# A graph network's closing layer: batch statistics taken about the first group's mean while the tiles are made, and the last norm's square and product on ScalarE with a bias and scale of each partition

## The reference, cut to what matters

```
h = (1.0 + eps[0]) * x + aggr                       # aggr: mean over incoming edges
out = jax.nn.relu(h @ w1 + b1) @ w2 + b2
out = out + (x @ res_w + res_b)
mean = jnp.mean(out, axis=0)                        # over the 6250 nodes, one for each feature
var = jnp.var(out, axis=0)
out = (out - mean) * jax.lax.rsqrt(var + BN_EPS) * gamma + beta
x = _layernorm(x + jax.nn.relu(out), axis=-1)       # _layernorm: (x - m) / sqrt(v + 1e-5) over the 128 features
```

## Time and profile before

| | us |
|---|---|
| median of 3 runs | 8809.26 |
| lowest, highest | 8806.7, 8819.43 |
| the profiled execution, own time | 8815.13 |
| its span, first to last instruction | 8813.4 |

### The profile page before, as it was taken

How to read it: one execution, slowest core, us unless ns; L and a number is a source line. 1 busy time by engine, 2 the same in 40 slices (tenths; PEclk the granted TensorE clock), 3 DMA queues, 4 the chain that set the end, 5 groups by cost and what they waited for, 6 DMA issues and landing times. The chain is left out here.

```text
span 8813.4 us, 60467 instructions
## 1 busy us (share of the span) xinstructions
PE 2052.3 (23%) x16367; PEld 1898.9 (22%) x16367; DVE 5593.5 (63%) x10159; ACT 3091.3 (35%) x3341; POOL 6086.1 (69%) x6351
## 2 busy tenths in 40 slices
PE   5776634555400000810000720000500000300002
PEld 5666634555300000710000610000400000200002
DVE  7665546766599998868888468888632222432225
ACT  6333312333266665345555345555200000100002
POOL 2777777777777775667776367777267776577773
PEclk5555555555555555955555865555555555555556
DMA  4621114444366665656665556666333332233331
GB/s 131 216 60 42 37 51 134 130 133 135 115 204 219 218 216 180 206 195 216 216 216 201 170 192 216 216 216 211 93 95 105 105 105 95 78 106 105 105 105 56
DMA packets 496250, 1288.01 MB, mean 146 GB/s; under 512 B 153909, under 2 KB 262024, under 8 KB 428968
## 3 DMA queue, kind: packets, MB, share of 16 engines
q1 hardware_dynamic: 236712, 755.83, 24.3%
q0 software_dynamic: 229248, 473.78, 18.5%
q10 hardware_dynamic: 29952, 54.54, 2.4%
HBM read 731.68 MB, written 551.98 MB: 146 GB/s over the span
## 5 line engine op out<-in xcount | busy, mean ns | idle before, releaser
L1405 POOL DMA_INDIRECT l_swp_G<-table,KVI x1664 | 1576.4, 947 | 512.3 <-issue 506.7
L1661 POOL DMA_INDIRECT l2s_G<-table,OTHI x832 | 786.7, 946 | 388.1 <-issue 253.3
L1661 POOL DMA_INDIRECT l3s_G<-table,OTHI x832 | 787.7, 947 | 301.5 <-issue 253.3
L1065 POOL DMA_INDIRECT arrived<-plc_QS,plc_idx x832 | 812.3, 976 | 253.5 <-issue 244.3
L1065 POOL DMA_INDIRECT slots<-REC,plc_idx x832 | 798.5, 960 | 273.1 <-issue 251.7
L1150 POOL DMA_INDIRECT l_G<-table,OTHI x832 | 790.1, 950 | 256.1 <-issue 253.0
L904 PE MATMUL plc_pr<-plc_seen,plc_otf 128*128 128x49 f32 x3328 | 861.5, 414 | 12.4 <-DVE plc_seen L674 12.4
L904 PEld LDWEIGHTS plc_pr<-plc_seen,plc_otf 128*128 128x128 f32 x3328 | 846.6, 326 | 32.1 <-issue 31.9
L1508 DVE SCALAR_TENSOR_TENSOR l_swp_QS<-l_swp_QS,KEEP,l_swp_QX 128x128 f32<-128x128 f32 x1664 | 588.3, 354 | 45.9 <-DMA l_swp_QX<-queries 8.6
L1617 PE MATMUL l_swp_AW<-l_swp_ET,ones 128*128 128x512 f32 x4 | 4.1, 1140 | 2155.2 <-DVE l_swp_ET L1597 2155.2
L1287 DVE TENSOR_TENSOR_SCAN l_X<-l_AW,l_X 128x2244 f32<-128x2244 f32 x104 | 502.5, 4831 | 3.6
(11 more groups left out here) (491 smaller groups left out, 9633.2 us busy)
## 6 DMA issues: line engine op xcount, KB each, us to landing
sums<-l_ROW SPq DMA_DIRECT2D x104, 1088.0 KB, 4.6
l_swp_QX<-queries SPq DMA_DIRECT2D x104, 1088.0 KB, 8.3
sums<-l_swp_ROW SPq DMA_DIRECT2D x104, 1088.0 KB, 5.2
queries<-plc_zrow SPq DMA_DIRECT2D x55, 1088.0 KB
plc_QX<-queries SPq DMA_DIRECT2D x104, 544.0 KB, 4.2
l_A<-arrived SPq DMA_DIRECT2D x52, 1056.0 KB, 7.7
sums<-l3s_ROW SPq DMA_DIRECT2D x52, 1032.0 KB
plc_low<-low_rows ACTq DMA_DIRECT2D x208, 256.0 KB, 3.6
```

The lines of the kernel that those rows point to most:

```text
L1065: pool.indirect_dma_start(out=slots, out_offset=bass.IndirectOffsetOnAxis(ap=idx[:, c % IB, j:j + 1], axis=0), in_=g.REC[:, c * CH + j, :] ...
L1405: pool.indirect_dma_start(out=G[:, c % GR, j, :], out_offset=None, in_=table, in_offset=bass.IndirectOffsetOnAxis(ap=index[:, c * CK + j:c ...
L1661: pool.indirect_dma_start(out=G[:, c % GR, j, :], out_offset=None, in_=table, in_offset=bass.IndirectOffsetOnAxis(ap=g.OTHI[:, c * CK + j: ...
```

## The change

Batch statistics. TensorE's sum of every tile in the loop (L2660) is kept for the first seven tiles only; their sum, divided by 7 x 128, is the mean of the first group (the same PSUM bank, now read as pp). From step 7 on, once in seven steps, VectorE adds its negative to one group of HH (part(G), between keep and mix; the first also reads pp), ScalarE squares that group at the head of its next step (square(G)), and TensorE, at the end of the step after, sums both the shifted group and its squares (total(G), 14 matmuls). The seventh group's part, square and total stand behind the loop. The variance is then the mean of the squares less the square of the mean, both about the shifted origin, and gamma, beta and the remaining mean are folded into one scale and one offset for each feature.

The last norm. VectorE's group-wide subtraction (L2581) and product (L2590) go. ScalarE squares tile by tile with the negative mean as a bias of each partition (seven instructions for a group), and multiplies tile by tile with Identity, scale and bias of each partition (seven more). VectorE gets one small operation more in second(G), and first(G) begins, from G = 2, with a wait for the norm of group G-2.

```
@@ names and buffers @@
...
-        stat = s.sb("stat", [P, 2, D])
-        st = s.sb("st", [P, 2, 3, GT])
+        stat = s.sb("stat", [P, 4, D])
+        st = s.sb("st", [P, 2, 4, GT])
+        pp = pm
@@ sync @@
-                sp.wait_ge(normed, G + 1)
+                sp.wait_ge(normed, (G + 1) * GT)
@@ -2551,43 +2553,54 @@
                 v.wait_ge(done, n + 1)
                 v.tensor_tensor(HH[:, n, :], po[:, n % 2, 0:D], g.RES[:, n, :], ALU.add).then_inc(kept, 1)
+            def part(G):
+                if G == 0:
+                    v.wait_ge(pivoted, 1)
+                    link(v.tensor_scalar(stat[:, 0, :], pp[:, 0:D], -1.0 / (GT * P), None, ALU.mult))
+                v.tensor_tensor(HH[:, group(G), :], HH[:, group(G), :], flat(stat[:, 0, :]), ALU.add).then_inc(parted, 1)
             for q in range(GT):
                 mix(q)
             for s_ in range(-3, NB):
                 if 0 <= s_ + 1 < NB:
                     keep(s_ + 1)
+                if s_ >= GT and (s_ + 1) % GT == 1 and s_ // GT - 1 < NG - 1:
+                    part(s_ // GT - 1)
                 mix(s_ + 3 + GT)
-            v.wait_ge(totalled, 1)
-            link(v.tensor_scalar(stat[:, 0, :], pm[:, 0:D], 1.0 / N, None, ALU.mult))
             v.wait_ge(kept, NB)
-            for G in range(NG):
-                v.tensor_tensor(HH[:, group(G), :], HH[:, group(G), :], flat(stat[:, 0, :]), ALU.subtract).then_inc(parted, 1)
+            part(NG - 1)
             v.wait_ge(varied, 1)
-            v.tensor_scalar(stat[:, 1, :], pv[:, 0:D], 1.0 / N, 1e-5, ALU.mult, ALU.add).then_inc(ready, 1)
+            link(v.tensor_scalar(stat[:, 2, :], pm[:, 0:D], 1.0 / N, None, ALU.mult))
+            link(v.tensor_tensor(stat[:, 3, :], stat[:, 2, :], stat[:, 2, :], ALU.mult))
+            link(v.tensor_scalar(stat[:, 1, :], pv[:, 0:D], 1.0 / N, 1e-5, ALU.mult, ALU.add))
+            v.tensor_tensor(stat[:, 1, :], stat[:, 1, :], stat[:, 3, :], ALU.subtract).then_inc(ready, 1)
             v.wait_ge(rooted, 1)
             link(v.reciprocal(stat[:, 1, :], stat[:, 1, :]))
             link(v.tensor_tensor(stat[:, 1, :], stat[:, 1, :], par[:, 0, :], ALU.mult))
+            link(v.tensor_tensor(stat[:, 2, :], stat[:, 2, :], stat[:, 1, :], ALU.mult))
+            link(v.tensor_tensor(stat[:, 2, :], par[:, 1, :], stat[:, 2, :], ALU.subtract))
             def first(G):
                 h, x, m = HH[:, group(G), :], g.X[:, group(G), :], st[:, G % 2, :, :]
-                if G == 0:
-                    v.wait_ge(squared, NG)
+                if G >= 2:
+                    v.wait_ge(normed, (G - 1) * GT)
                 link(v.tensor_tensor(h, h, flat(stat[:, 1, :]), ALU.mult))
-                link(v.tensor_tensor(h, h, flat(par[:, 1, :]), ALU.add))
+                link(v.tensor_tensor(h, h, flat(stat[:, 2, :]), ALU.add))
                 link(v.scalar_tensor_tensor(out=x, in0=h, scalar=0.0, in1=x, op0=ALU.max, op1=ALU.add))
                 link(v.tensor_reduce(m[:, 0, :], x, AX.X, ALU.add))
-                link(v.tensor_scalar(m[:, 0, :], m[:, 0, :], -1.0 / D, None, ALU.mult))
-                v.tensor_tensor(x, x, cols3(m[:, 0, :]).to_broadcast(wide), ALU.add).then_inc(centered, 1)
+                v.tensor_scalar(m[:, 0, :], m[:, 0, :], -1.0 / D, None, ALU.mult).then_inc(centered, 1)
             def second(G):
-                x, m = g.X[:, group(G), :], st[:, G % 2, :, :]
-                v.wait_ge(squared2, G + 1)
+                m = st[:, G % 2, :, :]
+                v.wait_ge(squared2, (G + 1) * GT)
                 link(v.tensor_reduce(m[:, 1, :], SQ[:, G % 2, :, :], AX.X, ALU.add))
                 v.tensor_scalar(m[:, 1, :], m[:, 1, :], 1.0 / D, 1e-5, ALU.mult, ALU.add).then_inc(spread, 1)
                 v.wait_ge(rooted2, G + 1)
                 link(v.reciprocal(m[:, 2, :], m[:, 2, :]))
-                v.tensor_tensor(x, x, cols3(m[:, 2, :]).to_broadcast(wide), ALU.mult).then_inc(normed, 1)
+                v.tensor_tensor(m[:, 3, :], m[:, 0, :], m[:, 2, :], ALU.mult).then_inc(scaled, 1)
             for G in range(NG + 1):
                 if G < NG:
@@ -2598,7 +2611,16 @@
         @block.scalar
         def _(act):
             act.wait_ge(loaded, 96)
+            def square(G):
+                act.wait_ge(parted, G + 1)
+                if G >= 2:
+                    act.wait_ge(totalled, G - 1)
+                act.activation(SQ[:, G % 2, :, :], HH[:, group(G), :], ACT.Square).then_inc(squared, 1)
             for s_ in range(-3, NB):
+                if s_ >= GT + 1 and s_ % GT == 1 and s_ // GT - 1 < NG - 1:
+                    square(s_ // GT - 1)
                 n = s_ + 3
                 if n < NB:
                     act.wait_ge(turned, n + 1)
@@ -2611,20 +2633,29 @@
                     if n >= 2:
                         act.wait_ge(done, n - 1)
                     act.activation(zt[:, n % 2, :], pz[:, n % 2, 0:P], ACT.Relu, bias=b1[:, 0:1]).then_inc(bent, 1)
-            for G in range(NG):
-                act.wait_ge(parted, G + 1)
-                if G >= 2:
-                    act.wait_ge(totalled, G)
-                act.activation(SQ[:, G % 2, :, :], HH[:, group(G), :], ACT.Square).then_inc(squared, 1)
+            square(NG - 1)
             act.wait_ge(ready, 1)
             act.activation(stat[:, 1, :], stat[:, 1, :], ACT.Sqrt).then_inc(rooted, 1)
+            def squares(G):
+                act.wait_ge(centered, G + 1)
+                for j in range(GT):
+                    act.activation(SQ[:, G % 2, j, :], g.X[:, G * GT + j, :], ACT.Square,
+                                   bias=st[:, G % 2, 0, j:j + 1]).then_inc(squared2, 1)
+            def norm(G):
+                act.wait_ge(scaled, G + 1)
+                for j in range(GT):
+                    act.activation(g.X[:, G * GT + j, :], g.X[:, G * GT + j, :], ACT.Identity,
+                                   bias=st[:, G % 2, 3, j:j + 1], scale=st[:, G % 2, 2, j:j + 1]).then_inc(normed, 1)
             for G in range(NG + 1):
                 if G < NG:
-                    act.wait_ge(centered, G + 1)
-                    act.activation(SQ[:, G % 2, :, :], g.X[:, group(G), :], ACT.Square).then_inc(squared2, 1)
+                    squares(G)
                 if G >= 1:
                     act.wait_ge(spread, G)
                     act.activation(st[:, (G - 1) % 2, 2, :], st[:, (G - 1) % 2, 1, :], ACT.Sqrt).then_inc(rooted2, 1)
+                    norm(G - 1)
         @block.tensor
         def _(pe):
@@ -2633,6 +2664,13 @@
             def ones_of(n):
                 return g.ones if n < NB - 1 else valid
+            def total(G):
+                pe.wait_ge(squared, G + 1)
+                for n in range(G * GT, (G + 1) * GT):
+                    pe.matmul(pm[:, 0:D], ones_of(n)[:, :], HH[:, n, :], start=(n == 0), stop=(n == NB - 1))
+                    o = pe.matmul(pv[:, 0:D], ones_of(n)[:, :], SQ[:, G % 2, n % GT, :], start=(n == 0), stop=(n == NB - 1))
+                o.then_inc(totalled if G < NG - 1 else varied, 1)
             for s_ in range(-3, NB):
                 n = s_ + 3
@@ -2655,17 +2693,14 @@
                         pe.wait_ge(kept, n - 1)
                     pe.matmul(po[:, n % 2, 0:D], zt[:, n % 2, :], w[:, 1, :], start=True, stop=True).then_inc(done, 1)
                 n = s_
-                if n >= 0:
+                if 0 <= n < GT:
                     pe.wait_ge(kept, n + 1)
-                    o = pe.matmul(pm[:, 0:D], ones_of(n)[:, :], HH[:, n, :], start=(n == 0), stop=(n == NB - 1))
-            o.then_inc(totalled, 1)
-            for n in range(NB):
-                G = n // GT
-                if n % GT == 0:
-                    pe.wait_ge(squared, G + 1)
-                o = pe.matmul(pv[:, 0:D], ones_of(n)[:, :], SQ[:, G % 2, n % GT, :], start=(n == 0), stop=(n == NB - 1))
-                if n % GT == GT - 1:
-                    o.then_inc(totalled if n < NB - 1 else varied, 1)
+                    o = pe.matmul(pp[:, 0:D], g.ones[:, :], HH[:, n, :], start=(n == 0), stop=(n == GT - 1))
+                    if n == GT - 1:
+                        o.then_inc(pivoted, 1)
+                if s_ >= GT + 2 and s_ % GT == 2 and s_ // GT - 1 < NG - 1:
+                    total(s_ // GT - 1)
+            total(NG - 1)
 class Args:
```

More of the change, by code:

```diff
@@ L2474, in close_all @@
             "chain", "loaded", "made_v", "mixed", "turned", "copied", "made", "bent", "done", "kept", "totalled"))
-        parted, squared, varied, ready, rooted, centered, squared2, spread, rooted2, normed, stored = (s.sem(x) for x in (
-            "parted", "squared", "varied", "ready", "rooted", "centered", "squared2", "spread", "rooted2", "normed", "stored"))
+        parted, squared, varied, ready, rooted, centered, squared2, spread, rooted2, normed, stored, pivoted, scaled = (
+            s.sem(x) for x in ("parted", "squared", "varied", "ready", "rooted", "centered", "squared2", "spread", "rooted2",
```

(1 more changed line is left out.)

## The result

The changed kernel takes 8840.1 us (median of 7 runs, 8838.19 to 8843.5) against 8807.19 us before (7 runs), a ratio of 1.0037, 95% interval 1.0028 to 1.0046: 33 us slower. The forecast was 8836, +26.6 us. The profiled execution took 8843.5 us with a span of 8841.8, against 8813.4.

A forecast was written before the change was run, and what follows sets the result against it. GpSimd's fetches were taken to bound the kernel up to 8716 us, then close_all's chain of waits. Terms 20.1 - 7.1 + 11.6 + 2 gave +26.6 us, the median going from 8809.3 to 8836, range 8814 to 8853.

The forecast's parts named there:

- rival 1: Making stage hides its additions, TensorE's total running under VectorE's mixes: 8814 us, no change that can be measured; chance 0.13.
- Rivals 2 and 4: 2: first(G)'s wait falls under other work, 8789 us, chance 0.03. 4: Identity forces function table loads, 8854 us, chance 0.04.
- Term 1: Making stage: in-order queues behind square and total stretch a cycle to 11.7 us, last keep at 8752.3; +20.1 us.
- term 4: TensorE's clock in the making stage: one total falling under the low clock costs 0 to 3.1 us; put at +2.
- Rival 3: Clock stays at 0.50 for most of the making stage, a cycle near 15 us: 8868, half of it 8852; chance 0.10.
- Term 2: Statistics, from the last keep to the last norm: 9.1 us where it was 16.2; -7.1 us.
- Term 3: Last norm: squares, Sqrt and norm form a chain with nothing beside it, 10.5 us a group against 8.5; +11.6 us.

The follow-up runs named there:

- the statistics alone: The change's batch statistics with the last norm of before, against the kernel before on the same chip: ratio 1.0035 (1.0006 to 1.0065), +26.8 us from the third group's first mix.

## Why the prediction was right

**In short.** The order of the queues was read rightly in both halves; one term, the clock, was sized wrong; and that the total came so near was part luck. The stage lost 36.4 us where the sum had 26.6, and the medians are only 33 apart; what makes up the 3.5 between isn't shown.

**What bounds, and the rivals.** The stage left the fetches' pace and was bound by its own order from the first part on, as said: mixes of the third group on came 14.8, 14.1, 13.3 and 14.0 us apart in the first result, and all of rival 1 is refuted by its own mark (the next group's first mix started 14.8 us behind its forerunner, not 8.7). Rivals 2 and 4 did not occur; the trace has no table load in close_all, and from the end of Sqrt to the first product are 0.47 us, which leave no room for one of 1.283.

**Term 1, the making stage.** Mechanism right, each hop of the cycle of rows above within 0.1 us but one: the total. The step that was off is term 4, the clock: one fall at +2 us, where every total in the loop met the low level, 29.7 us in place of 18.7. That is 11 us of the 11.9 by which the stretch passed 20.1. Its own signs say the same: VectorE's idle time was to be 2.5 to 3.5 us and was 4.8 to 5.7 behind every total; the last keep was to be near 8752, 87.6 us behind the first mix, and was 99.5 behind it. Rival 3 (the low clock for most of the stage) had the right cause and too high a price: from the first part to the last keep the clock was low for 31 of 77 us. The forecast had the warning in its hand, one block and longer gaps, and weighed it as a single accident.

**Term 2, the statistics.** -5.4 for -7.1: the last total took 5.0 us, at a granted clock of 0.66, where the first total of the statistics alone, at 1.00, took 3.3; the rest as counted. Without that the stretch is 9.2 us in four of the experiments, against 9.1 worked out.

**Term 3, the last norm.** +9.8 for +11.6. The prices were right (squares 2.15 for 7, one starting every 0.29; products 2.80 for 7, one every 0.39 with scale and bias), and so were both waits, 2.87 for norm and 1.12 for Sqrt. (The 0.09 for an operand came from two rows that differ also in the input's type, bf16 against f32; the 0.29 and 0.39 measured here bear it out.) The period was 10.26 for 10.5, some hops of 0.04 and a link counted too many. The experiments show both causes by taking them away: 2.96 us a group for the buffers, 1.22 for the new order on both engines. The rule of the Trainium skill to keep adding and multiplying on VectorE ("ScalarE: Activation LUTs", Rules for kernel authors) held for the change as made, and not once the order was right: there the move pays 2.4 us a group (8.51 to 6.08), since it empties the engine that bounds the stage.

## What to carry to other kernels

In hand-ordered queues a cheap instruction costs what stands behind it: ask for each block of work moved into a pipelined loop which engine's next step waits for its end, and cut it to the size of a step. Before an operation is moved to an idle engine, ask which instruction of the engine it left awaits its result, and how many buffers lie between: here two buffers in place of seven turned a gain of 5 us into a loss of 10, and the order of both queues gave another 5.5. When a block of matmuls lands behind a thinner stretch, as here, add up the sum at the lower clock too: 11 of 12 blocks met it.

## What was not expected of the hardware

The clock fell in or just ahead of nearly every block of 28 passes in the changed stage (11 of 12 in the two profiles of it), and came back within the block; filling the gaps held it at 1.00. What it looks at stays open. In the later runs every kernel took 17% longer, and from the second group on until the fetches had ended, hand-offs from TensorE to ScalarE and VectorE took up to 7.3 us, against 0.04 us afterwards and in the making stage of the first result, while those to TensorE took 0.05 us throughout. The cause was not looked for, and nothing above rests on it.
